# Storing the last three rows with twelve indexed GpSimd transfers instead of three plain SyncE transfers

## The reference, cut to what matters

```python
h = layernorm(x) * (1 + ca) + sa
x = x + ga * attn(h)              # mLSTM block, gated, scanned over the 512 tokens
h = layernorm(x) * (1 + cb) + sb
x = x + gb * ffn(h)               # 8 experts, top 2 of them per token, 128 -> 256 -> 128
return x
```

## Time and profile before

| | before |
|---|---|
| device time, median of 3 runs | 406.63 us (406.2 to 408.18) |
| span of the profiled execution, first to last instruction | 409.5 us |
| PE busy | 368.5 us, 90% of the span |
| DVE busy | 287.2 us, 70% |
| ACT busy | 230.6 us, 56% |
| POOL busy | 184.2 us, 45% |
| stores | 8 transfers of 256 KB, all from SP |

### The profile page before, as it was taken

One profiled execution on the slowest core, in us unless ns is written; L12 is line 12 of the kernel. 1 busy time (PEld: TensorE's weight loads), 2 busy tenths in 40 slices (PEclk: granted clock), 3 DMA queues, 4 the chain that ended last, 5 costly groups with the idle time before them and its releaser, 6 DMA issues.

```text
span 409.5 us, 6042 instructions
## 1 busy us (share of the span) xinstructions
PE 368.5 (90%) x1744; PEld 266.4 (65%) x1744; DVE 287.2 (70%) x786; ACT 230.6 (56%) x412; POOL 184.2 (45%) x180
## 2 busy tenths in 40 slices
PE   3915987999999999999999999999999999897995
PEld 2804875767576767776677757775777667574663
DVE  3797558688657986688567976797558975756553
ACT  1500243576466848476556756685647675575673
POOL 7892071167233654266324743375214641464130
PEclk9975799999799989999699999998799999999998
DMA  4920000000000000000000000000000000000000
GB/s 117 293 61 1 2 2 0 1 2 0 2 1 26 0 0 0 26 0 0 0 26 0 0 0 5 21 0 0 0 26 2 0 0 29 0 0 2 26 2 26
DMA packets 8965, 7.10 MB, mean 17 GB/s; under 512 B 1195, under 2 KB 7510, under 8 KB 8950
## 3 DMA queue, kind: packets, MB, share of 16 engines
q1 hardware_dynamic: 8722, 6.78, 5.7%
q10 hardware_dynamic: 164, 0.07, 0.1%
q0 software_dynamic: 64, 0.07, 0.1%
HBM read 4.82 MB, written 2.10 MB: 17 GB/s over the span
## 4 chain that ended last, share of the span: by engine, by line
PE 71%; DVE 14%; issue 6%; ACT 3%; POOL 3%; DMA 1%; SPq 0%; DVEq 0%; POOLq 0%
PE bank L956 8%; PE bank L984 7%; PE bank L958 6%; PE bank L957 6%; PE bank L994 6%; PE bank L974 6%; PE bank L975 6%; PE bank L926 5%; PE bank L911 2%; DVE hg_lo L774 2%; PE bank L859 2%; DVE m_row L741 2%; PE bank L933 2%; PE bank L836 2%; PE bank L874 2%
## 5 line engine op out<-in xcount | busy, mean ns | idle before, releaser
L763 DVE TENSOR_TENSOR hg<-hid,bank 128x512 f32<-128x512 f32 x128 | 86.8, 682 | 72.1 <-PE bank L994 45.5
L476 ACT ACTIVATE hid<-bank,cols 128x512 f32<-128x512 f32 x128 | 87.8, 686 | 86.0 <-PE bank L958 85.3
L424 POOL TENSOR_TENSOR hg_lo<-hg,hg_hi 128x512 fp32r<-128x512 f32 x69 | 90.2, 1309 | 98.2 <-ACT hg_hi L494 98.1
L494 ACT ACTIVATE hg_hi<-hg 128x512 fp32r<-128x512 f32 x128 | 79.6, 622 | 10.4 <-DVE hg L763 10.4
L956 PE MATMUL bank<-h_hi,w_hi 128*128 (+1 forms) x128 | 61.5, 481 | 0.0
L984 PE MATMUL bank<-hg_lo,w_hi 128*128 128x512 f32 x128 | 53.4, 417 | 1.1 <-DVE hg_lo L774 0.9
L974 PE MATMUL bank<-hg_hi,w_hi 128*128 128x512 f32 x128 | 52.7, 412 | 0.0
L957 PE MATMUL bank<-h_hi,w_lo 128*128 (+1 forms) x128 | 51.7, 404 | 0.0
L958 PE MATMUL bank<-h_lo,w_hi 128*128 (+1 forms) x128 | 51.7, 404 | 0.0
L975 PE MATMUL bank<-hg_hi,w_lo 128*128 128x512 f32 x128 | 51.7, 404 | 0.0
L393 POOL TENSOR_SCALAR var_eps<-mv 128x4 f32<-128x4 f32 x16 | 4.5, 278 | 98.4 <-DVE mv L555 98.4
(11 more groups left out here) (162 smaller groups left out, 618.1 us busy)
## 6 DMA issues: line engine op xcount, KB each, us to landing
out_dram<-x_all SPq DMA_DIRECT2D x8, 256.0 KB, 2.3
w_raw<-in_L_ffn_W_dram SPq DMA_DIRECT2D x1, 1024.0 KB, 8.6
x_all<-in_L_attn_x_dram SPq DMA_DIRECT2D x2, 256.0 KB, 4.4
wmod_sb<-in_L_wmod_dram SPq DMA_DIRECT2D x1, 384.0 KB, 5.2
vo_raw<-in_L_attn_Wv_dram POOLq DMA_DIRECT2D x1, 32.0 KB, 2.3
qk_raw<-in_L_attn_Wq_dram ACTq DMA_DIRECT2D x1, 32.0 KB, 2.9
vo_raw<-in_L_attn_Wo_dram POOLq DMA_DIRECT2D x1, 32.0 KB, 3.6
qk_raw<-in_L_attn_Wk_dram ACTq DMA_DIRECT2D x1, 32.0 KB, 3.2
```

Source lines behind the costliest of these rows:

```text
L424: g.tensor_tensor(hg_lo[k][:, :], hg[k][:, :], hg_hi[k][:, :].bitcast(fp32), ALU.subtract).then_inc(s_lo_pool, 1)
L476: a.activation(hid[n % 4][:, :], up_bank[n % 2][:, :], ACT.Relu, bias=cols[:, R_B1 + n:R_B1 + n + 1]).then_inc(s_hid, 1)
L494: a.activation(hg_hi[k][:, :], hg[k][:, :], ACT.Copy).then_inc(s_hghi, 1)
L763: v.tensor_tensor(hg[k][:, :], hid[k][:, :], gate_bank[n // NU % 2][:, :], ALU.mult).then_inc(s_hg, 1)
```

## The change

The loop on SP stores rows 0 to 4 only. Rows 5, 6 and 7 are stored from POOL, each in four indexed transfers of 128 DRAM rows of 512 B: transfer j takes block j of the row in SBUF, and for each partition an index in `row_ix` says which row of the output, seen as 4096 rows of 128 features, it goes to. `row_ix` is made once by an `iota` among POOL's first instructions. The stores of rows 5 and 6 stand at t = 12 of turns 6 and 7, where POOL's next work is the `hg_lo` of step 11 in turn 6 and of step 12 in turn 7; the store of row 7 is POOL's last work. SP's last wait takes in the twelve transfers.

```diff
+        row_ix = sb("row_ix", [P, 3 * NT], u32)
...
+        s_rowix = sem("s_rowix")
+        s_out_ix = sem("s_out_ix")
...
+        out_rows = out.rearrange("b t d -> (b t) d")
...
-            with sp.Fori(0, B) as b:
+            with sp.Fori(0, B - 3) as b:
                 sp.wait_ge(s_o, b + 1)
                 sp.dma_start(out_v[bass.ds(b, 1)].rearrange("b p j d -> p (b j) d"),
                              row(x_all, b).rearrange("p (j d) -> p j d", j=NT)).then_inc(s_out, 16)
-            sp.wait_ge(s_out, 16 * B)
+            sp.wait_ge(s_out, 16 * (B - 3))
+            sp.wait_ge(s_out_ix, 16 * 3 * NT)
...
+            g.iota(row_ix[:, :], [[P, 3 * NT]], base=(B - 3) * T, channel_multiplier=1).then_inc(s_rowix, 1)
             pool.wait_ge(s_const, CONSTS)
+
+            def store(b):
+
+                pool.wait_ge(s_rowix, 1)
+                pool.wait_ge(s_o, b + 1)
+                for j in range(NT):
+                    c = (b - (B - 3)) * NT + j
+                    g.indirect_dma_start(out=out_rows, out_offset=bass.IndirectOffsetOnAxis(row_ix[:, c:c + 1], 0),
+                                         in_=x_all[:, b * T + j * P:b * T + (j + 1) * P], in_offset=None).then_inc(s_out_ix, 16)
...
             def body(b, end, start, ahead, live):
                 m1, m2 = b + 1, b + 2
                 for t in range(LAG, N + LAG):
+                    if t == 12 and not start:
+                        store(b - 1)
...
             last_turns(body)
+            store(B - 1)
```

## The result

The changed kernel takes 420.35 us (median of 4 runs, 418.9 to 422.04), the kernel before 407.4 us (median of 4, 406.2 to 410.04) in the same comparison. The ratio is 1.028, with a 95% interval of 1.0232 to 1.0329: slower, by 12.95 us between the medians and by 11.4 (9.5 to 13.4) by the ratio. The ratio uses only runs within 1.5% of the fastest of their kernel, a median all of them. The forecast was 411.9 with a range of 407.4 to 418.0. The direction was right and the size wrong: 5.3 us forecast, more than twice that measured.

What follows compares the result with a forecast made beforehand. PE was taken to bound the kernel, with stores costing nothing until the last. Delays of 0.81 (turn 6), 0.59 (turn 7) and 3.9 us (end) sum to 5.3, added to 406.63: 411.9 us, range 407.4 to 418.0.

Steps and rivals of the forecast that it cites:

- The three places and their covers: Row 5's store in turn 6 and row 6's in turn 7, partly covered, row 7's uncovered: 0.81, 0.59, 3.9 us.
- the start and the landing at the end: Row 7's store: POOL starts at about 406.7, right behind L794; landing 1.9 us after the last issue; 3.9 us later overall.
- The formulas: Delays: 4d - 3.59 in turn 6, 4d - 3.81 in turn 7, 4d - 0.5 at the end.
- 4d: POOL's time to issue the four indexed transfers of one row: 4.4 us.
- PE's waits: In turn 6 PE idles before L984 of step 11 for POOL's `hg_lo`, in place of 2.19 us before L966.
- POOL's order: Four issues come before `hg_lo` of step 11 in turn 6, of step 12 in turn 7, and behind L794 at the end.
- DVE's relief: Turn 6: with POOL on descriptors, DVE's `top_d` and `top_s` need not wait; `top_d` 0.1 to 0.2 us, no gain at 1.1.
- The term d: Time one indexed transfer of 128 rows occupies POOL: 1.1 us, twice the second load's; ends 0.54 and 1.52.
- the prediction's step from that rule to d = 0.54: If generating descriptors is small, as the skill says, an indexed issue on POOL would take 0.54 us.
- A (short issue): POOL's issue takes 0.54 us; gates let L966 come 0.9 early, the end costs 1.7; sum +0.8, 407.4 us; chance 0.13.
- B (issues hold DVE): Four issues in a row hold DVE: +2.8 in turn 6, +2.5 in turn 7, +3.9 at the end; 415.8 us; chance 0.17.
- C (indices are dear by their number): Reading 128 indices costs as much as writing descriptors or more: 2 us per transfer, 16.1 in all, 422.7 us; chance 0.15.

Runs made afterwards that it cites:

- the spare matmuls: Changed kernel plus 15 spare matmuls on PE where it waits for step 11's `hg_lo` in turn 6: 418.22 us, ratio 1.034; with 30 of them 419.71 us, 1.030.
- the second: The changed kernel measured again, unaltered, against the kernel before: 417.92 against 409.48 us, ratio 1.028 (1.014 to 1.042).
- the kernel with steps 3 and 4: Kernel before, stores untouched; in turn 6 POOL makes `hg_lo` of steps 3 and 4, DVE those of 12 and 13: 407.54 against 409.02 us, ratio 0.995.
- the run with 64 indices: Against the kernel before, only row 7 stored from POOL by indexed transfers, eight of 64 indices each: 422.03 us (one run) against 409.02.

## Why the prediction was wrong

**The three places and their covers were right; three terms were not.** Of the 3.7 us by which the stretches (9.03) exceed the forecast (5.3), 1.57 are the clock, which had no term, 1.66 are POOL's time for its transfers, and 0.45 the start and the landing at the end.

**What held.** The formulas, with POOL's measured time in place of 4d, give 5.13 - 3.59 = 1.54 for turn 6 without the clock, and 4.96 - 3.81 = 1.15 for turn 7. The measured values are 1.51 (3.08 less the 1.57 that the spare matmuls gave back) and 1.20. PE's waits, POOL's order and DVE's relief came as written.

**The term d was mis-sized, and for a wrong reason.** I had 1.1 as twice the rows of the second load. It is 1.26, of which the rows have no part: 0.54 for a plain transfer of 64 or of 128 rows, and 0.72 for the index (0.66 where 64 are read). That 1.1 came near is luck: the 0.54 that I added for the rows stands where the index's 0.72 belongs. In the two turns there is what I had left out, 0.16 to 0.18 before the first transfer and 0.17 more for the very first; the last of four has no gap of 0.30 behind it. So the three groups took 5.13, 4.96 and 4.77 us in place of 4.4 each, 1.66 more. At the end 0.79 us pass from row 7's result to POOL's first transfer, where I had 0.1; with plain transfers from POOL it was 0.57, from SyncE 0.18. Against that, 2.08 us lie behind the last issue, 0.25 less than for SyncE's. The end is thus 7.64 - 2.89 = 4.75 in place of 3.9. On the emission's cost the Trainium skill (DMA: Bandwidth & Descriptors, "Anatomy of one DMA — SWDGE (gpsimd) path") says that many descriptors can be emitted before it shows. The plain transfers agree (0.54 us with 128 pieces, 0.77 with 512), and the indexed ones don't tell against it: 64 pieces fewer make only 0.07 us. But the prediction's step from that rule to d = 0.54 left out the index.

**The granted clock was missing from the sum.** I let an idle wait cost its own length. The 3.6 us before step 11 cost 1.57 on top. The trace of before could have warned: its clock falls several times.

**The rest is spread, as far as it is known.** 9.3 us are accounted for, with the 0.3 outside the span; the first comparison said 11 to 13, the second 8.4 between its medians. Runs of the kernel before lie up to 11 us apart. By its own formula, 12d - 7.9, the measured d of 1.26 gives 7.2, or 413.9 us, and with all 9.3 it would be 415.9: both lie in the stated range. The last 4.4 us up to 420.35 are in no stretch. Of them 0.8 is the median of before, which its fourth run put at 407.4 in place of 406.63; the rest goes with the falls of the clock in the four runs, as argued above, and for these the range had no room.

**The rivals.** A (short issue): its d was wrong, and with plain transfers, which have that d, its gain didn't come either: the gates were 0.59 late, and the sum was +2.49 in place of +0.8. Gates 2.8 us sooner are real where POOL is off `hg_lo` for longer, as in the changed kernel, but there PE was late by `hg_lo`; the kernel with steps 3 and 4 collects part of them. B (issues hold DVE): refuted for indexed transfers, `top_d` took 0.16 us. That its price of 9.2 us is almost the 9.03 of the stretches is chance. C (indices are dear by their number): refuted by the run with 64 indices and by d, though its price for the whole, 16 us, was nearer to the first comparison than mine.

## What to carry to other kernels

Count transfers, not bytes or rows, when POOL issues them: here each indexed one occupied POOL for 1.1 to 1.3 us with 64 or 128 indices and with 512 B or 2 KB for each, against 0.54 for a plain one, so use few and wide ones, and put them where POOL is idle. A store that ends the kernel was cheapest here from SyncE in one piece. When an edit makes TensorE wait for 2 us or more, the slow matmuls behind the wait can come on top of its price (here 1.6 us), and when another engine's small operations end together with POOL's large ones, moving POOL's work is worth a try.

## What the runs showed of the hardware

- An indexed transfer has a gap of 0.30 us to the next on POOL; plain ones follow without a gap.
- POOL's indexed transfers are issued beside DVE's small operations without holding them (0.16 us). Beside four plain ones, one such operation took 0.88. POOL's `hg_lo` holds them for up to 1.25 us, and three `hg_lo` in a row held one for 2.86.
- The granted clock fell after 2.2 us of idle time in one profile of five, and after 3.6 us in three of three. Each of these falls cost about 1.6 us. The one of the five, and two of the three, had also fallen one turn earlier. Where it falls in the untouched turns differs from one execution to the next.
